# A gated cross-attention block on one core: product with V for two pairs at once, shift rows next to it, bias matmul over all rows, high part of the maxima on ScalarE

## The reference

```python
# x, ctx: (32, 256, 256); 16 heads of 16 dims
def xattn(query, key, value, ...):              # query = layernorm(x), key = value = ctx
    q, k, v = proj(query, Wq, bq), proj(key, Wk, bk), proj(value, Wv, bv)
    q = q * cos + rotate_half(q) * sin          # k likewise
    scores = einsum('bhqd,bhkd->bhqk', q, k) / sqrt(16)
    scores = where(|i - j| <= 50, scores, -1e9)
    p = softmax(scores)
    return einsum('bhqk,bhkd->bhqd', p, v) @ Wo.T + bo
x = x + tanh(g_xattn) * xattn(layernorm(x), ctx, ctx, ...)
x = x + tanh(g_ffn) * ffn(layernorm(x))         # ffn: quantised gate, up and down products, 768 wide
```

## Time and profile before

| what | us |
|---|---|
| median of 3 runs (lowest to highest) | 1427.61 (1423.87 to 1428.71) |
| profiled execution, its own time | 1429.06 |
| its span | 1427.3 |
| PE busy in the span | 1286.9 (90%) |
| DVE busy | 1213.0 (85%) |
| ACT busy | 835.7 (59%) |
| POOL busy | 585.8 (41%) |

### The profile page before, as it was taken

One profiled execution on the slowest core, in us unless ns is written; L12 is line 12 of the kernel. 1 busy time (PEld: TensorE's weight loads), 2 busy tenths in 40 slices (PEclk: granted clock), 3 DMA queues, 4 the chain that ended last, 5 costly groups with the idle time before them and its releaser, 6 DMA issues. The chain is left out here.

```text
span 1427.3 us, 27869 instructions
## 1 busy us (share of the span) xinstructions
PE 1286.9 (90%) x8992; PEld 837.0 (59%) x8992; DVE 1213.0 (85%) x3572; ACT 835.7 (59%) x1336; POOL 585.8 (41%) x1392
## 2 busy tenths in 40 slices
PE   3378999999999999999999886999899979987998
PEld 2256777767777777777777552444343334436887
DVE  4678898989899898989898744999799989997886
ACT  2225565656565666666566544665577679993332
POOL 1127777777777777777777650000000000000000
PEclk9969999999999999999999997999999999997999
DMA  3175656565656566665656400222455546556674
GB/s 111 41 152 122 162 133 158 135 157 138 153 142 149 142 150 146 147 152 147 146 148 148 103 31 30 110 102 96 147 185 186 177 166 198 191 180 198 228 242 162
DMA packets 132369, 207.27 MB, mean 145 GB/s; under 512 B 11159, under 2 KB 97050, under 8 KB 126106
## 3 DMA queue, kind: packets, MB, share of 16 engines
q1 hardware_dynamic: 132250, 205.86, 51.6%
HBM read 125.60 MB, written 79.69 MB: 144 GB/s over the span
## 5 line engine op out<-in xcount | busy, mean ns | idle before, releaser
L705 DVE CUSTOM_DVE_ANT_0 psum<-psum,band 128x178 f32<-128x178 f32 x1024 | 318.2, 371 | 40.8 <-PE psum L833 40.5
L589 ACT ACTIVATE probs<-psum 128x356 f32<-128x356 f32 x512 | 209.8, 463 | 232.4 <-PE psum L850 232.2
L520 POOL TENSOR_SCALAR_AFFINE_SELECT probs<-probs 128x154 f32<-128x154 f32 (+1 forms) x512 | 213.7, 426 | 169.1 <-ACT probs L589 164.2
L1008 PE MATMUL psum<-xnT,w_upT 128*128 (+1 forms) x1152 | 261.7, 385 | 18.9 <-DVE maxima L1232 8.8
L1008 PEld LDWEIGHTS psum<-xnT,w_upT 128*128 128x128 f16 x1152 | 109.9, 99 | 170.5 <-issue 33.4
L875 PE MATMUL psum<-probs,V 128*32 128x178 f32 x2048 | 206.8, 321 | 2.0 <-POOL probs L529 1.9
L529 POOL TENSOR_SCALAR_AFFINE_SELECT probs<-probs 128x254 f32<-128x254 f32 (+1 forms) x512 | 189.1, 393 | 0.0
L833 PE MATMUL psum<-k_stack,q_stack 96*128 96x178 bf16 x1024 | 129.9, 244 | 20.2 <-issue 7.3
L1608 PE MATMUL psum<-w_downT,xnT 128*128 128x256 f16 x1152 | 128.5, 276 | 15.9 <-DVE xnT L1558 15.9
L705 DVE DVE_READ_ACCUMULATOR2_ANT smax<- 128x1 f32 x1024 | 141.4, 138 | 0.0
L1008 PE MATMUL psum<-xnT,w_gateT 128*128 (+1 forms) x576 | 127.3, 385 | 8.8 <-DVE xnT L1081 8.8
(11 more groups left out here) (190 smaller groups left out, 2296.2 us busy)
## 6 DMA issues: line engine op xcount, KB each, us to landing
k_parts_scratch<-k_parts SPq DMA_DIRECT2D x32, 384.0 KB, 2.6
q_parts_scratch<-q_parts SPq DMA_DIRECT2D x32, 384.0 KB, 2.6
k_stack<-k_parts_scratch SPq DMA_DIRECT2D x32, 384.0 KB, 5.1
q_stack<-q_parts_scratch SPq DMA_DIRECT2D x32, 384.0 KB, 5.0
gate_scratch<-g_stage SPq DMA_DIRECT2D x16, 768.0 KB, 3.3
g_in<-gate_scratch SPq DMA_DIRECT2D x16, 768.0 KB, 4.6
sig_scratch<-w_gateT SPq DMA_DIRECT2D x32, 384.0 KB, 2.4
sig_again<-sig_scratch SPq DMA_DIRECT2D x32, 384.0 KB, 3.4
```

Of the source, the lines that this page charges most:

```text
L520: nc.gpsimd.affine_select(out=t[:, :, 0:n], in_=t[:, :, 0:n], pattern=[[0, 2], [1, n]], compare_op=ALU.is_ge, fill=0.0, base=WINDOW - off, ...
L589: nc.scalar.activation(ring_tile(probs, b, pair, c)[:].rearrange("p e j -> p (e j)"), scoreT_bank[c][:, 0:2 * SPAN], ACT.Exp, scale=DK ** ...
L705: ins = nc.vector.tensor_tensor_reduce(out=mine, in0=mine, in1=keep["band"][:, t, :], scale=1.0, scalar=-3e38, op0=ALU.add, op1=ALU.max, a ...
L1008: last = nc.tensor.matmul(bank[:], weights[wp][:, c * I + f * P:c * I + (f + 1) * P], x_parts[:, c, bass.ds(j * (2 * TILE) + xp * TILE, TI ...
```

## The change

V is kept without gaps: 17 columns for each head (16 of V and the 1), and the 32 columns that a product loads run on into the next head, whose results nobody reads. The tiles are therefore set to 1.0 by one memset each. The ring has eight tiles. `weigh` is called in odd slots only, for two pairs, one after the other. PE's `shift_rows` moves behind `scoresT`, directly ahead of the products with V. `shift_parts` is split: the high part is a copy on ACT (`shift_top`) at the start of slots 3 and 7, without the sign, the low part a subtraction on DVE (`shift_low`) behind the maxima of the slot, and `shift_copy` multiplies by -1. The bias matmul of the output projection works over 128 rows, of which 125 hold zeros.

```diff
-RING = 6
+RING = 8
+VCOL = DK + 1
...
-            nc.vector.memset(keep["ones3"][:], 1.0).then_inc(ones_set, 1)
+            nc.vector.memset(keep["ones"][:], 1.0).then_inc(ones_set, 1)
+            nc.vector.memset(keep["bias"][:], 0.0).then_inc(ones_set, 1)
...
-        V = bufs("V", [P, T * H, OUT])
+        V = bufs("V", [P, T * H * VCOL + OUT - VCOL])
...
+            def shift_top(b, half):
+                if not b.real:
+                    return
+                reached(act, max_taken, b, 2 * PAIRS, PAIRS * (half + 1))
+                reached(act, shift_transposed, b.before(1), HALVES, half + 1)
+                nc.scalar.activation(shift[:, :, half, 0, :], smax[b.buf][:, :, half * 8:half * 8 + 8], ACT.Copy)\
+                    .then_inc(shift_high, 1)
...
-                nc.scalar.activation(shiftT[half][:], shift_bank[half][0:SHIFT * 8, 0:S // 2].bitcast(BF16), ACT.Copy)\
-                    .then_inc(shiftT_copied, 1)
+                nc.scalar.activation(shiftT[half][:], shift_bank[half][0:SHIFT * 8, 0:S // 2].bitcast(BF16), ACT.Copy,
+                                     scale=-1.0).then_inc(shiftT_copied, 1)
...
                     if slot == 3:
+                        shift_top(b2, 1)
                         high(b0, "k")
...
                     if slot == 7:
+                        shift_top(b1, 0)
                         copy_out(b3, att_transposed, 1, 1, bank_a[:], attT[:].rearrange("p c t -> p (c t)"),
...
-            def shift_parts(b, half):
...
-                nc.vector.tensor_scalar(shift[:, :, half, 0, :], src, -1.0, None, ALU.mult).then_inc(shift_high, 1)
+            def shift_low(b, half):
                 reached(dve, shift_high, b, HALVES, half + 1)
-                nc.vector.scalar_tensor_tensor(shift[:, :, half, 1, :], src, -1.0, shift[:, :, half, 0, :],
-                                               ALU.mult, ALU.subtract).then_inc(shift_ready, 1)
+                nc.vector.tensor_tensor(shift[:, :, half, 1, :], smax[b.buf][:, :, half * 8:half * 8 + 8],
+                                        shift[:, :, half, 0, :], ALU.subtract).then_inc(shift_ready, 1)
...
                     if slot == 3:
-                        shift_parts(b2, 1)
                         rope(b0, "q", bank_a)
...
-                    if slot == 7:
-                        shift_parts(b1, 0)
                     pair, late = pair_at(slot, S_FIRST)
                     maxima(Batch(rnd, unit, late), pair)
+                    if slot == 3:
+                        shift_low(b2, 1)
+                    if slot == 7:
+                        shift_low(b1, 0)
...
-                    nc.tensor.matmul(bank[:], keep["ones3"][:], keep["bias"][:], start=True, stop=True,
+                    nc.tensor.matmul(bank[:], keep["ones"][:], keep["bias"][:], start=True, stop=True,
...
+                        v_at = (c * H + h // 2 + PAIRS * (h % 2)) * VCOL
...
-                                                V[b.buf][:, c * H + h // 2 + PAIRS * (h % 2), :], ring_tile(probs, b, pair, c)[:, e, :],
+                                                V[b.buf][:, v_at:v_at + OUT], ring_tile(probs, b, pair, c)[:, e, :],
...
-                    if slot == 3:
-                        if b3.real:
-                            reached(pe, out_normed, b3, HALVES, 1)
-                        shift_rows(b2, 1)
...
-                        shift_rows(b1, 0)
                     pair, late = pair_at(slot, ST_FIRST)
                     scoresT(Batch(rnd, unit, late), pair)
-                    pair, late = pair_at(slot, PV_FIRST)
-                    weigh(Batch(rnd, unit, late), pair, b2)
+                    if slot == 3:
+                        if b3.real:
+                            reached(pe, out_normed, b3, HALVES, 1)
+                        shift_rows(b2, 1)
+                    if slot == 7:
+                        shift_rows(b1, 0)
+                    if slot % 2 == 1:
+                        for back in (1, 0):
+                            pair, late = pair_at(slot - back, PV_FIRST)
+                            weigh(Batch(rnd, unit, late), pair, b2)
```

More of the change, by code:

```diff
@@ L146, in _ @@
             sp.dma_start(keep["band"][:], dram["band"]).then_inc(consts_in, 16)
+            sp.wait_ge(ones_set, 3)
             sp.wait_ge(part_step, 5)
@@ L233, in _ @@
         def _(pe):
-            pe.wait_ge(ones_set, 6)
+            pe.wait_ge(ones_set, 7)
             for k, blks in enumerate(plan):
@@ L397, in run, with v_heads @@
                 steps(it // NBUF, it % NBUF)
+        def v_heads(buf):
+            return V[buf][:, 0:T * H * VCOL].rearrange("p (h d) -> p h d", d=VCOL)
         def pair_at(slot, first):
@@ L627, in steps @@
                         if b0.n == 0:
-                            act.wait_ge(consts_set, 2 * NBUF)
+                            act.wait_ge(consts_set, NBUF)
                         if b0.real:
                             copy_out(b0, projected["v"], 1, 1, bank_b[:].rearrange("p (h d) -> p h d", d=DK),
-                                     V[b0.buf][:, :, 0:DK], v_copied, [(weighted, b0.before(NBUF), PAIRS, PAIRS)])
+                                     v_heads(b0.buf)[:, :, 0:DK], v_copied, [(weighted, b0.before(NBUF), PAIRS, PAIRS)])
                         middle(b0, "q")
@@ L656, in _ @@
             for k in range(NBUF):
[L657 to L662, removed]
+                nc.vector.memset(V[k][:], 1.0).then_inc(consts_set, 1)
             def statistics(b, src, st, mom, taken, aggregated):
@@ L708, in maxima @@
                     ins.then_inc(max_taken, 1)
-            def shift_parts(b, half):
+            def shift_low(b, half):
                 if not b.real:
                     return
-                reached(dve, max_taken, b, 2 * PAIRS, PAIRS * (half + 1))
-                reached(dve, shift_transposed, b.before(1), HALVES, half + 1)
-                src = smax[b.buf][:, :, half * 8:half * 8 + 8]
-                nc.vector.tensor_scalar(shift[:, :, half, 0, :], src, -1.0, None, ALU.mult).then_inc(shift_high, 1)
                 reached(dve, shift_high, b, HALVES, half + 1)
-                nc.vector.scalar_tensor_tensor(shift[:, :, half, 1, :], src, -1.0, shift[:, :, half, 0, :],
-                                               ALU.mult, ALU.subtract).then_inc(shift_ready, 1)
+                nc.vector.tensor_tensor(shift[:, :, half, 1, :], smax[b.buf][:, :, half * 8:half * 8 + 8],
+                                        shift[:, :, half, 0, :], ALU.subtract).then_inc(shift_ready, 1)
             def divide(b, half):
@@ L1661, in build @@
             keep["ident"], keep["identb"] = sba("ident", [P, P]), sba("identb", [P, P], BF16)
-            keep["ones3"], keep["bias"] = sba("ones3", [3, P], BF16), sba("bias", [3, T * D], BF16)
+            keep["ones"], keep["bias"] = sba("ones", [P, P], BF16), sba("bias", [P, T * D], BF16)
             keep["qk_bias"] = sba("qk_bias", [P, 4])
```

## The result

| kernel | median, us (lowest to highest) | ratio to before, 95% interval |
|---|---|---|
| before | 1428.2 (1423.9 to 1429.5) | |
| after | 1471.2 (1469.8 to 1472.1) | 1.031 (1.028 to 1.033) |

The change makes the kernel 43 us slower.

A forecast was written before the change was run, and what follows sets the result against it. Neither PE nor DVE alone was taken as the bound, but a path changing between engines. 1.80 us more a pass over 30 passes (54 us) gave 1482, and clock falls of 24 us made 1506, range 1463 to 1542.

The forecast's parts named there:

- the stall less the savings: Slot 3 wait and other path costs minus PE's savings: 1.80 us more a pass, 54 us over 30 passes.
- the clock: PE's clock falls to 1.2 GHz after idle time in slot 3, in two passes of three: 24 us.
- rotation of Q to M(3): From DVE's rotation of Q to its four maxima of slot 3: 1.57 us, unchanged.
- M(3) to M(4): From DVE's maxima of slot 3 to those of slot 4: 3.55 us, 1.58 more, behind the low part.
- M(6) to bias matmul: From DVE's maxima of slot 6 to the output projection's bias matmul: 2.39 us, 0.1 less.
- end of the projection to S(0): From the output projection's end to the score products of slot 0 on PE: 2.34 us, 0.48 more.
- KP to rotation of Q: From PE's projection of K to DVE's rotation of Q: 6.21 us, 0.33 more.
- the second adds 0.58 to 0.60: On PE, a second V product block right behind the first costs 0.58 to 0.60 us of its own.
- Rival (a): The slot 3 stall comes as worked out, but the clock holds at 2.4 GHz: 1482 us; chance 0.30.
- rival (b): The clock falls in every pass and falls or lasts through slot 7 too: 1560 us; chance 0.08.
- Rival (d): Gains and the stall cancel within 4 us; chance 0.03.
- Rival (c): PE is the only bound and its savings of 1.37 us a pass count in full: 1387 us; chance 0.07.

The follow-up runs named there:

- e1: Changed kernel with 13 extra matmuls filling PE's idle time in slot 3, between the transposed scores and the transposes of shift rows; 1437.4 us, ratio 1.006.
- e2: Changed kernel with the product with V called in every slot for one pair, as before the change; 1459.3 us, ratio 1.020.
- e6: e3 with the low part of Q on POOL in slot 5 moved ahead of the band cut; 1394.7 us, ratio 0.976.
- e8: e4 with the low part of Q on POOL in slot 5 moved ahead of the band cut; 1395.6 us, ratio 0.977.
- e9: e7 with the bias matmul back on 3 rows; 1392.6 us, ratio 0.973.
- e3: Changed kernel with DVE's low part of the shift in slot 3 moved ahead of the maxima; 1416.0 us, ratio 0.990.
- e4: Kernel before with only the V products for two pairs in odd slots, ring of eight and V in 17 columns; 1409.7 us, ratio 0.987.
- e5: e3 with ACT's attT copy ahead of the high part in slot 7; 1414.3 us, ratio 0.989.
- e10: e7 with the transposes of shift rows in slots 3 and 7 ahead of the transposed scores again; 1380.9 us, ratio 0.967.
- e7: e3 with e5's edit, and on POOL in slot 5 the low part of Q ahead of the scales and band cut; 1375.4 us, ratio 0.963.

## Why the prediction was right, and where it was not

The direction was right, and both parts of the mechanism came: PE's stall behind the low part in slot 3, and the clock's falls after it. The time was inside the range, 35 us under the figure given. But the two big terms were both mis-sized, and the errors went against each other. The forecast gave 54 us to the stall less the savings and 24 to the clock; e1 gives the first about nothing and leaves the 43 us to the clock. That the sum stayed in the range is in part luck: with the first term as e1 measured it (a pass 0.1 longer than before, so 3 us) and the clock's 24 as forecast, the sum is about 1455, an estimate, and that is under the range's low end.

| step, us | forecast | measured |
|---|---|---|
| rotation of Q to M(3) | 1.57 | 1.58 (402.82 to 404.40), 2.12 (e1, median at full clock) |
| M(3) to M(4) | 3.55 | 3.02 (e1, full clock; median 2.68), 3.97 (after; median 3.64) |
| M(6) to bias matmul | 2.39 | 2.2 |
| end of the projection to S(0) | 2.34 | 1.77 (419.43 to 421.20) |
| M(0) to KP | 1.50 | 1.54 (395.64 to 397.18) |
| KP to rotation of Q | 6.21 | 5.64 (397.18 to 402.82) |
| pass without the clock | 25.3 | 23.4 to 23.6 (e1) |
| clock, a pass | 0.8 | 1.4 to 1.6 |

**The step that failed: "the second adds 0.58 to 0.60".** Sixteen matmuls of two pairs last 0.83 (399.78), no longer than eight, and the next work starts 0.76 after them, for 0.73 with one pair. The term sits three times on the path, and 3 x 0.57 = 1.7 us is as much as the difference between 25.3 and 23.6; the errors of the other terms cancel. The largest of those is in the place of M(3): it waits for S(3) and q_stack, so that in e1's median the rotation of Q to M(4) takes 4.91 us, 0.21 under the 5.12 of the forecast and not 0.57. The row that it rested on, 1.38 for sixteen matmuls at 844.27, stood in the tail of the pipeline. There the second block had waited for POOL's band cut, whose line in the kernel before is this:

```profile
844.10 0.69 POOL L529 TENSOR_SCALAR_AFFINE_SELECT probs<-probs 128x254 f32<-128x254 f32 x2
```

It ends at 844.79, and the ninth of the sixteen matmuls began at 844.84, released by this line. The row had no wait in brackets, since a merged row shows only the wait before its first instruction. The trace shows each fp32 product as two matmuls, so a pair has eight. One pair's two heads use two of the four groups of 32 columns, and two pairs use all four. The Trainium skill (TensorE: Matmul & The Clock Gate, "Part 3: Packing small matmuls") says that products in different column groups run at the same time in the array; the 0.83 agrees, and by that rule the forecast without the clock would have been near the 1428 of before, an estimate.

**The stall in slot 3** came as worked out: 1.16 for the maxima, 0.62 at 405.56 for the low part (0.50 was taken; it ran beside POOL's rotation), and S(4) behind it. PE's idle time was 0.75 and 1.70, 2.45 together, for a forecast of 2.2 in one piece. The part of it before S(3) was missed: the text had the q_stack loads off the path. PE waits for them in the kernel after, and that idle time helped to bring the clock down (e2). In the pass shown DVE's path misses the wait, but as soon as the pass is shorter M(3) waits with it: 0.55 us in e1's median.

**The clock** was the other mis-sized term. Taken were falls in two passes of three at 1.2 us; there were falls in every pass, at 1.4 to 1.6. Rival (a), the clock at 2.4 GHz throughout, is refuted by all 27 passes and by e1. No single idle time of PE in the 27 passes is longer than 2.2, and the clock fell in all of them. The Trainium skill (TensorE: Matmul & The Clock Gate, "Why this matters for your kernels") advises against idle gaps of more than about 3 us; by it the clock would have stayed, so here the advice is not enough. Of rival (b), with a chance of 0.08, the first half came, a fall in every pass; its second half, falls in slot 7, did not in the kernel after, but did in e6, e8 and e9. Rival (d), that gains and stall cancel, had 0.03; e1 shows just that for the part without the clock. Rival (c), faster by PE's savings, comes in part once the low part stands ahead of the maxima: e3's pass at full clock is 1.0 us shorter than before, of the 1.37 that (c) counted.

**The small terms.** M(6) to the bias matmul, with the high part ahead of the attT copy, was booked as a gain of 0.1 and was 0.3. The high part is a loss even so: pairs alone bring this stretch to 1.62 (e4), with the high part ahead of the copy it is 2.18 (e1, e3), and behind it 1.57 (e5). So the term hid a gain of 0.9 from pairing and a cost of 0.6. The bias term was 0.09 and is 0.25 (e9). The shift rows were 0.40 and are 0.20 on the path (e10). The loads of V, 17 columns apart, take 110 ns in the median in both kernels. What DVE saves was off the path, as said: e7, which has the saving, is 0.45 shorter at full clock than e8, which has not, and the bias (0.25) and the shift rows (0.20) account for that.

## What to carry over

When an instruction is moved behind another on one engine, write down what the consumers' in-order lists hold behind the wait: here the low part of a shift, 0.2 us of work, held two pairs of products and the next scores. Count PE's idle times and not only its work, since a pass that is shorter or emptier can lose its clock: e5 took 0.6 us out of a pass and got no time for it, and e1 added work and won 34 us. Look also where in the pass the clock falls and not only how often, since e8 has as many falls as e4, in another place. Read the price of a merged row only where nothing can have waited inside it.

## What the runs showed of the hardware

Four heads' products on four groups of 32 columns take PE as long as two heads' on two (0.83 in the kernel after, 0.80 before and in e2). A bias matmul over 3 rows costs 0.21 to 0.25 us more than one over 128 rows, 125 of them zero (e9 against e7), of which only 0.09 can be read at the matmul itself, in the median. An idle time of PE of 1.65 us before the transposes, with 0.10 ahead of it, went with a low clock in 5 passes of 27 (e2); 1.55 with 0.94 ahead of it in 27 of 27 (after). No run here varied the distance between the two at the same sum. The clock also fell in slot 7 in passes without an idle time over 0.5 us there (e6, e8, e9). The low part, a subtraction of 128x16 on DVE, lasted 0.62 us in slot 3 and ended at 406.18, with POOL's addition of 128x512 that ran from 404.88 to 406.14; in slot 7 of the same pass it lasted 0.17 (after).
